# The experts' first layer in two fp16 parts, with a power-of-two scale of the weights formed on the chip

## The reference, cut to what matters

```python
logits = xt @ gate_w.T + gate_b
scores = softmax(logits); top_w, top_i = top_k(scores, 2)
def expert(w1e, b1e, w3e, b3e, w2e, b2e):          # each 256 x 256, 8 experts
    h = silu(xt @ w1e.T + b1e) * (xt @ w3e.T + b3e)
    return h @ w2e.T + b2e
y = sum over the two experts of a row, weighted by top_w
z = silu(xt @ ws1.T + bs1) * (xt @ ws3.T + bs3) @ ws2.T + bs2
```

## Time and profile before

| | |
|---|---|
| time, median of 3 runs | 591.88 us (591.18 to 594.17) |
| profiled execution: time, span | 593.51 us, 591.5 us |
| PE busy in the span | 562.3 us (95%) |
| PEld | 465.1 us (79%) |
| DVE | 452.1 us (76%) |
| ACT | 376.6 us (64%) |
| POOL | 257.5 us (44%) |
| mean granted TensorE clock | 0.984 |
| expert loop | 188 to 357 us |

### The profile page before, as it was taken

How to read it: one execution, slowest core, us unless ns; L and a number is a source line. 1 busy time by engine, 2 the same in 40 slices (tenths; PEclk the granted TensorE clock), 3 DMA queues, 4 the chain that set the end, 5 groups by cost and what they waited for, 6 DMA issues and landing times.

```text
span 591.5 us, 12910 instructions
## 1 busy us (share of the span) xinstructions
PE 562.3 (95%) x3942; PEld 465.1 (79%) x3942; DVE 452.1 (76%) x1246; ACT 376.6 (64%) x729; POOL 257.5 (44%) x291
## 2 busy tenths in 40 slices
PE   7989999999999999999999999979889999999997
PEld 7777998888879999999999997866646655655664
DVE  4778888886864877778888873757989899878765
ACT  5376887677634877777677753255575784785643
POOL 4427555565470234455443335667544651410100
PEclk9598999999999999999999999999999999999999
DMA  8225434562158878879998827453122330200000
GB/s 238 86 90 196 153 140 155 197 235 109 52 183 265 295 249 257 283 238 275 282 278 275 277 96 287 153 204 90 37 62 73 111 121 37 73 1 37 37 37 35
DMA packets 47973, 93.15 MB, mean 157 GB/s; under 512 B 6990, under 2 KB 17306, under 8 KB 47778
## 3 DMA queue, kind: packets, MB, share of 16 engines
q1 hardware_dynamic: 39740, 74.34, 37.5%
q0 software_dynamic: 7440, 17.97, 10.1%
q10 hardware_dynamic: 726, 0.02, 0.1%
HBM read 61.32 MB, written 32.17 MB: 158 GB/s over the span
## 4 chain that ended last, share of the span: by engine, by line
PE 61%; DVE 19%; ACT 9%; issue 6%; POOL 3%; DMA 1%; ACTq 0%; DVEq 0%; POOLq 0%; SPq 0%
PE bank L1363 13%; PE bank L1364 12%; PE bank L1365 12%; PE bank L1870 6%; PE bank L1301 4%; PE bank L1891 3%; PE bank L1893 3%; POOL yr L756 2%; DVE st L2447 2%; DVE xa L2438 2%; DVE g3l L2524 2%; DVE sl L2519 2%; DVE x L2081 2%; PE bank L1307 1%; PE bank L1330 1%
## 5 line engine op out<-in xcount | busy, mean ns | idle before, releaser
L660 POOL DMA_INDIRECT rows_by_expert<-n,pos x64 | 64.4, 1006 | 49.2 <-DVE pos L2175 32.7
L708 POOL TENSOR_TENSOR yg<-yg,b 128x512 f32<-128x512 f32 x31 | 45.9, 1481 | 89.6 <-ACT yg L848 89.6
L756 POOL DMA_INDIRECT yr<-expert_out,out_row x64 | 65.7, 1026 | 29.3 <-issue 19.0
L1363 PE MATMUL bank<-xTh,wph 128*128 128x256 f32 x248 | 72.3, 291 | 0.3 <-issue 0.2
L1870 PE MATMUL bank<-m4Th,wint 128*128 128x512 f16 x192 | 69.1, 380 | 2.6 <-DVE sl L2519 2.6
L1365 PE MATMUL bank<-xTh,wpl 128*128 128x256 f32 x248 | 70.1, 283 | 0.0
L1364 PE MATMUL bank<-xTl,wph 128*128 128x256 f32 x248 | 70.0, 282 | 0.0
L1870 PE MATMUL bank<-m4Tl,wint 128*128 128x512 f16 x192 | 68.8, 379 | 0.0
L2340 DVE TENSOR_TENSOR wpl<-wraw,wph 128x1024 fp32r<-128x1024 f32 x40 | 49.0, 1224 | 11.1 <-ACT wph L848 11.0
L848 ACT ACTIVATE wph<-wraw 128x1024 fp32r<-128x1024 f32 x40 | 42.4, 1059 | 14.6 <-PE bank L1365 9.7
L1363 PEld LDWEIGHTS bank<-xTh,wph 128*128 128x128 f32 x248 | 47.2, 190 | 0.6 <-issue 0.6
(11 more groups left out here) (352 smaller groups left out, 1727.1 us busy)
## 6 DMA issues: line engine op xcount, KB each, us to landing
wraw<-in_wexp SPq DMA_DIRECT2D x40, 512.0 KB, 4.6
xg<-rows_by_expert SPq DMA_DIRECT2D x31, 256.0 KB, 4.1
expert_out<-yg SPq DMA_DIRECT2D x31, 256.0 KB, 3.3
x_shared<-x SPq DMA_DIRECT2D x8, 512.0 KB, 3.1
xa<-x_shared SPq DMA_DIRECT2D x4, 1024.0 KB, 6.8
out<-ost SPq DMA_DIRECT2D x8, 512.0 KB, 2.7
xin<-in_x SPq DMA_DIRECT2D x7, 512.0 KB, 3.7
stage<-in_wexp SPq DMA_DIRECT2D x8, 256.0 KB, 3.6
```

The source lines that it names most:

```text
L660: pool.indirect_dma_start(out=xs, out_offset=bass.IndirectOffsetOnAxis(ap=pos[p][:, k, j:j + 1], axis=0), in_=n2[p][:, j, :], in_offset=No ...
L708: pool.tensor_tensor(yg[u % 3], yg[u % 3], b2[:, bass.ds(e, 1), :].broadcast_to([P, 2, D]), ALU.add)\
L756: pool.indirect_dma_start(out=yr[:, c, k, j, :], out_offset=None, in_=ys, in_offset=bass.IndirectOffsetOnAxis(ap=out_row[:, b * GB + c, k, ...
L1363: mm(o, ah, bh, start=first, stop=False)
```

## The change

`hidden(u)` gets both operands as fp16 parts. The rows are scaled by 2^11 (an immediate) and each expert's weights by a power of two, so that the largest stays within fp16 and the low parts don't vanish; the scale is taken off again in the silu's `scale` operand, in the split of `hb`, or for singles in `gated`. `outp` stays float32r. The scale comes from the mean square of an expert's first-layer weights: every expert's `wraw` is loaded once more, early, into one of two buffers `early`, and squared with an accumulated sum on ScalarE, one in steps 1 and 2 and two in steps 3, 4 and 5; TensorE sums over partitions in `biases()`, POOL raises to -0.5, VectorE keeps the exponent bits and forms the tables `wscale`, `unscale` and `b3c`. ScalarE and VectorE read the unit's expert before the weights' cast, no longer before silu and gate.

```diff
+        early = Area(area_a, top).put("early", [P, 2, KD, 2 * F], F32)
-        wph = [wa.put(f"wph{p}", [P, KD, 2 * F], F32R) for p in range(2)]
-        wpl = [wa.put(f"wpl{p}", [P, KD, 2 * F], F32R) for p in range(2)]
+        wph = [wa.put(f"wph{p}", [P, KD, 2 * F], F16) for p in range(2)]
+        wpl = [wa.put(f"wpl{p}", [P, KD, 2 * F], F16) for p in range(2)]
...
-        xTh = [ct.put(f"xTh{p}", [P, KD * P2], F32R) for p in range(2)]
+        xTh = [ct.put(f"xTh{p}", [P, KD * P2], F16) for p in range(2)]
...
+        def early_of(g):
+            return range(g - 1, g) if g < 3 else range(2 * g - 4, 2 * g - 2) if g < 6 else range(0)
...
                 if load:
                     load_x(g + 2, p)
+                for at, e in enumerate(early_of(g)):
+                    if early_of(g)[0]:
+                        sp.wait_ge(sem("norm_step"), early_of(g)[0])
+                    src = i["wexp"][e * (3 * P):e * (3 * P) + 2 * P, :].rearrange("(k p) n -> p k n", k=KD)
+                    sp.dma_start(early[:, at], src).then_inc(sem("early_in"), 16)
                 store_mid(g - 1, 1 - p)
...
                 scatter(f, 1 - p, (1,), second)
+                if g == 6:
+                    pool.wait_ge(sem("setup_copied"), 8)
+                    pool.tensor_scalar(wpow, wsum, SMALLEST, None, ALU.max).then_inc(sem("norm_step"), 1)
+                    pool.wait_ge(sem("norm_step"), NE + 1)
+                    pool.tensor_tensor(wpow, wpow, halfpow[:, 0:NE], ALU.pow).then_inc(sem("norm_step"), 1)
...
                 expert_high(g)
+                for at, e in enumerate(early_of(g)):
+                    act.wait_ge(sem("early_in"), 16 * (early_of(g)[-1] + 1))
+                    w = early[:, at].rearrange("p k n -> p (k n)")
+                    act.activation(w, w, ACT.Square, accum_out=wsq[:, e:e + 1]).then_inc(sem("norm_step"), 1)
...
             def weights_high(u):
+                at = tile_slot(u)
+                experts[u] = act.value_load(tile_expert[0:1, at:at + 1], min_val=0, max_val=NE - 1)
...
-                copy(wph[u % 2], wraw[u % 3]).then_inc(sem("high_done0"), 1)
+                copy(wph[u % 2], wraw[u % 3], scale_of(wscale, experts[u])).then_inc(sem("high_done0"), 1)
...
+            act.wait_ge(sem("table_done"), 1)
+            act.wait_ge(sem("norm_step"), NE + 4)
             weights_high(0)
...
-                copy(xTh[u % 2][:, 0:n], bank[:, 4 + u % 2, 0:n]).then_inc(sem("xTh_done"), 1)
+                copy(xTh[u % 2][:, 0:n], bank[:, 4 + u % 2, 0:n], ROW_SCALE).then_inc(sem("xTh_done"), 1)
...
-                        act.activation(hb[u % 2][:, n], bank[:, 2 * (u % 2), n], ACT.Silu,
+                        act.activation(hb[u % 2][:, n], bank[:, 2 * (u % 2), n], ACT.Silu, scale=scale_of(unscale, e),
...
-                    copy(hTh[u % 2], hb[u % 2]).then_inc(sem("hTh_done"), 1)
+                    copy(hTh[u % 2], hb[u % 2], scale_of(unscale, experts[u])).then_inc(sem("hTh_done"), 1)
...
                 pe.wait_ge(sem("shared_done"), pairs(5))
+                pe.wait_ge(sem("norm_step"), NE)
+                mm(bank[:, piece_bank(5, 0), 4 * NE:5 * NE], mean_of, wsq, start=True, stop=True)
...
+                if g == 7:
+                    dve.wait_ge(sem("norm_step"), NE + 2)
+                    chained(ts(wpow.bitcast(I32), wpow.bitcast(I32), EXPONENT, None, ALU.bitwise_and))
+                    chained(ts(wscale, wpow, LARGEST, None, ALU.mult))
+                    chained(ts(wpow, wscale, ROW_SCALE, None, ALU.mult))
+                    dve.reciprocal(unscale, wpow).then_inc(sem("norm_step"), 1)
+                    stt(b3c, b13c[:, 2:4, :], ROW_SCALE, wscale.unsqueeze(1).broadcast_to([P, 2, NE]), ALU.mult, ALU.mult)
...
-                tt(wpl[u % 2], wraw[u % 3], wph[u % 2], ALU.subtract).then_inc(sem("low_done0"), 1)
+                stt(wpl[u % 2], wraw[u % 3], scale_of(wscale, experts[u]), wph[u % 2], ALU.mult, ALU.subtract)
...
-                tt(xTl[u % 2][:, 0:n], bank[:, 4 + u % 2, 0:n], xTh[u % 2][:, 0:n], ALU.subtract).then_inc(sem("xTl_done"), 1)
+                stt(xTl[u % 2][:, 0:n], bank[:, 4 + u % 2, 0:n], ROW_SCALE, xTh[u % 2][:, 0:n], ALU.mult, ALU.subtract)
...
-                    tt(hTl[p], hb[p], hTh[p], ALU.subtract).then_inc(sem("hTl_done"), 1)
+                    stt(hTl[p], hb[p], scale_of(unscale, experts[u]), hTh[p], ALU.mult, ALU.subtract).then_inc(sem("hTl_done"), 1)
```

More of the change, by code:

```diff
@@ L35 @@
 HID_SCALE = 2.0 ** -19
+LARGEST = 2.0 ** 15 / 16
+SMALLEST = 1e-30
+EXPONENT = 0x7F800000
 ALU = mybir.AluOpType
@@ L105, in flamingo_kernel @@
         row_gap = keep.put("row_gap", [NE, 1], F32)
-        b13c = keep.put("b13c", [P, 4, NE], F32)
+        b13c = keep.put("b13c", [P, 5, NE], F32)
+        wsum = b13c[:, 4, :]
         incl = keep.put("incl", [NE, NE], F32)
@@ L130, in flamingo_kernel @@
         tile_row = keep.put("tile_row", [1, 2, NU], I32)
+        wsq = keep.put("wsq", [P, NE], F32)
+        wpow = keep.put("wpow", [P, NE], F32)
+        wscale = keep.put("wscale", [P, NE], F32)
+        unscale = keep.put("unscale", [P, NE], F32)
+        b3c = keep.put("b3c", [P, 2, NE], F32)
         area_a = keep.at
+        early = Area(area_a, top).put("early", [P, 2, KD, 2 * F], F32)
         wa = Area(area_a, top)
         wraw = [wa.put(f"wraw{p}", [P, KD, 2 * F], F32) for p in range(3)]
-        wph = [wa.put(f"wph{p}", [P, KD, 2 * F], F32R) for p in range(2)]
-        wpl = [wa.put(f"wpl{p}", [P, KD, 2 * F], F32R) for p in range(2)]
+        wph = [wa.put(f"wph{p}", [P, KD, 2 * F], F16) for p in range(2)]
+        wpl = [wa.put(f"wpl{p}", [P, KD, 2 * F], F16) for p in range(2)]
         wa.at = area_a + 2 * NE * KD * 2 * F * 4
@@ L212, in flamingo_kernel @@
         xg = [t.bitcast(F32) for t in xgr]
-        xTh = [ct.put(f"xTh{p}", [P, KD * P2], F32R) for p in range(2)]
-        xTl = [ct.put(f"xTl{p}", [P, KD * P2], F32R) for p in range(2)]
+        xTh = [ct.put(f"xTh{p}", [P, KD * P2], F16) for p in range(2)]
+        xTl = [ct.put(f"xTl{p}", [P, KD * P2], F16) for p in range(2)]
         hb, hbr = zip(*(ct.put_turned(f"hb{p}", [P, 2 * F]) for p in range(2)))
@@ L846, in _, with copy @@
         def _(act):
-            def copy(dst, src):
-                return act.activation(dst, src, ACT.Copy)
+            def copy(dst, src, scale=1.0):
+                return act.activation(dst, src, ACT.Copy, scale=scale)
             def stage_high(c, dst, n):
@@ L964, in biases_copy @@
                 act.wait_ge(sem("setup_mm"), 5)
-                copy(b13c.rearrange("p m e -> p (m e)"), bank[:, piece_bank(5, 0), 0:4 * NE]).then_inc(sem("setup_copied"), 1)
+                copy(b13c.rearrange("p m e -> p (m e)"), bank[:, piece_bank(5, 0), 0:5 * NE]).then_inc(sem("setup_copied"), 1)
             def step(g, p, nxt=True):
@@ L1032, in _, with scale_of @@
             f = NG - 1
+            experts = {}
+            def scale_of(table, e):
+                return table[:, bass.ds(e, 1)]
             def weights_high(u):
+                at = tile_slot(u)
+                experts[u] = act.value_load(tile_expert[0:1, at:at + 1], min_val=0, max_val=NE - 1)
                 act.wait_ge(sem(f"stage_in{u % 3}"), 16 * (EARLY[u % 3] + u // 3 + 1))
@@ L2336, in tile_tables, with scale_of @@
                         .then_inc(sem("table_done"), 1)
+            experts = {}
+            def scale_of(table, e):
+                return table[:, bass.ds(e, 1)]
             def weights_low(u):
+                at = tile_slot(u)
+                experts[u] = dve.value_load(tile_expert[0:1, at:at + 1], min_val=0, max_val=NE - 1)
                 dve.wait_ge(sem("high_done0"), EARLY[0] + u + 1)
-                tt(wpl[u % 2], wraw[u % 3], wph[u % 2], ALU.subtract).then_inc(sem("low_done0"), 1)
+                stt(wpl[u % 2], wraw[u % 3], scale_of(wscale, experts[u]), wph[u % 2], ALU.mult, ALU.subtract)\
+                    .then_inc(sem("low_done0"), 1)
             hidden(f, 0)
@@ L2357, in _ @@
             route_c(f)
+            dve.wait_ge(sem("table_done"), 1)
+            dve.wait_ge(sem("norm_step"), NE + 4)
             weights_low(0)
```

16 lines of the change are left out of this document (9 added, 7 removed).

## The result

The changed kernel takes 606.35 us (median of six, 601.12 to 607.97) where the one before takes 591.8 (median of six, 589.59 to 594.17): 1.0231 times as long, 95% interval 1.0196 to 1.0267. The forecast was 590.4, in a range up to 596.5; slower was given 0.20.

The account below looks back on a forecast made before the run. TensorE was taken to bound the expert loop, ScalarE's path to `probsT` the shared steps. Squares +6.05, clock +1.6, loop start +0.15 and matmuls -9.3 sum to -1.5 us: 590.4 from 591.88, range 586.5 to 596.5.

Parts of the forecast that it names:

- What bounds the kernel: Expert loop: TensorE sets the pace, matmuls 91.4% of the chain; shared steps: the path runs through ScalarE's `probsT`.
- Part 1, matmuls: Expert loop: fp16 hidden matmuls start every 0.1093 us, not 0.120; -9.3 us in all, bounds -9.9 and -7.8.
- Part 1, "Does another engine become the bound?": Expert loop: TensorE stays the bound; in a triple of about 11.15 us VectorE stands at 10.2, ScalarE near 9.8.
- Part 1, register loads: Expert loop: reads of the expert's number, moved ahead of the weight casts, run while their engine works; nobody waited there.
- Part 1, pointer operands: Expert loop: `[P,1]` operands cost ScalarE 0.09 us each, 0.36 per pair unit; VectorE's two between 0 and 0.09 each.
- Part 2, squares: End of steps 1 to 5 on ScalarE: eight squares of 1.05 us, after slack +6.05 us (5.0 to 7.5).
- Part 3, clock: Steps 4 to 6: longer TensorE idles bring two clock falls at 0.8 us each, +1.6 us (0 to 5.1).
- Part 4, "covered work", early loads: Shared steps: eight loads of 512 KB, queued on SP before `store_mid`, land half a step before their square; no cost.
- The wait of TensorE in `biases()`: Step 6: work behind the last square ends at 126.2 us, before `probsT` at 126.9; uncovered it would be 1.5 us.
- The expert loop doesn't follow TensorE: Rival, expert loop: late `wraw` landings hold triples at 11.81 us; 595.8, or 599.8 if all is held; chance 0.1.
- A table load for the square: Rival, shared steps: squares need their own table, five more loads of 1.28 us, +6.4 less slack; 596.4; chance 0.06.
- fp16 between fp32r matmuls: Rival, expert loop: fp16 streams no faster alternating with fp32r, gain 0 to 2 us; 598 to 600; chance 0.04.

Follow-up runs that it names:

- const_imm: const with immediates in place of pointer operands and the register loads back where they were before; 584.87 us, 0.9893 of before.
- const: The changed kernel without early loads, squares, product and power, scale tables filled with constants, register loads and pointer operands kept; 591.59 us, 0.9998 of before.
- const_reg: const, but ScalarE reads the expert of unit u + 2 ahead of silu_of(u), not behind it; 588.09 us, 0.9939 of before.
- squares: const plus the eight squares at the end of steps 1 to 5, on the data of only two early loads; 604.05 us, 1.0216 of before.
- warm8: The changed kernel with 8 spare products that TensorE issues in steps 2 to 6 while it waits for probsT; 616.50 us, 1.0283 of before.
- loads: const plus the eight early loads of 512 KB at their places in the steps, with no square reading them; 598.50 us, 1.0135 of before.
- first_dve: const, but a single's silu comes behind the next weights' cast on ScalarE, and VectorE reads the expert earlier; 596.68 us, 0.9925 of before.
- best: The changed kernel with squares in ScalarE's waits, loads behind the second norm, early register reads, singles' next cast ahead of silu; 596.34 us, 0.9933 of before.

## Why the prediction was wrong, point by point

- *The whole.* By the stretches, the result lies 15.3 us above the forecast: 9.9 in the loop, 5.0 in steps 1 to 6, 0.4 in the other two, the start left aside. Of the 5.0, squares are 2.2 (8.3 for 6.05), the clock 2.0 (3.6 for 1.6) and the last 0.8 fits step 3, where the wait for scatters is.
- *What bounds the kernel.* Right for before: TensorE paces the loop. Right too that the steps hang on ScalarE ahead of `probsT`.
- *Part 1, matmuls.* Right: 0.109 us apart, a pair unit 4.35 (forecast 4.38), and const_imm shows that triples can do better than the 11.15 forecast.
- *Part 1, "Does another engine become the bound?"* This is the step that failed in the loop. The prediction added up each engine's busy time in a triple (VectorE 10.2, ScalarE 9.8 of 11.15) and found slack. The true limit was a path through both, gate sum to silu to cast to low part to rows' low part, which had 1.22 us of slack in before; a TensorE faster by 0.7 to 1.1 a triple and a path longer by 0.70 use that up. Forecast -9.3, measured 0 (const); moving the register load alone gave 3.6 back (const_reg).
- *Part 1, register loads.* "They run in the queue while their engine works, and where they stood nobody waited": wrong, 0.38 us behind each single's silu. A load runs ahead only as far as the wait in front of it allows.
- *Part 1, pointer operands.* Right in size: `wph` 1.15 for 1.06, silu 0.56 for 0.47, `wpl` 1.28 for 1.22. They belong on the path, not in the busy sum.
- *Part 2, squares.* The length was right (1.04 for 1.05). This is the step that failed in the shared part: most of the slack taken off in steps 3 to 5 wasn't there. squares' step 3 grew by 2.1 us for its two squares, after's step 4 by 1.6, so nearly all of the 8.3 us count where 6.05 were taken; squares measured 12.8 with its falls. I read the reason from the order of work, and no run tests it: a step's start, values, residual, norm, softmax and next step's start close a circle, so a delay stays, and what looks early in one step of before is early only against a step that wasn't delayed.
- *Part 3, clock.* Two falls, as forecast, but some 1.8 us each and not 0.8: about 3.6 for 1.6, within the bounds given. The size is what steps 5 and 6 grew by beyond their squares; warm8 didn't settle it.
- *Part 4, "covered work", early loads.* Wrong: the loads were taken at 0, alone they cost 8 us (loads), and in after they show as 1.9 us of waits. I looked at which queue issued them and when they were wanted, not at whose transfers they stand beside. The wait of TensorE in `biases()` was 1.6 us, the "uncovered" value, and part of the idle ahead of step 6's fall.
- *Sums.* The lower bound of the matmuls' gain adds up to -10.1 us and not -9.9 (7.2, 1.2 and 1.7), and triples that keep 11.81 us for 11.15 would take back 5.9 and not 5.4. Neither decides anything.
- *Rivals.* "The expert loop doesn't follow TensorE" had the right outcome for the loop and the wrong mechanism: no wait for `wraw` in after's triples. It became true in const_imm, first_dve and best, where the ring was shortened. A table load for the square did not come, and fp16 between fp32r matmuls was fast. The time lay above all of them, because each assumed that only one half failed.

## What to carry to other kernels

When the engine that sets the pace gets faster, don't compare the others' busy sums with the new period: follow one item from engine to engine and compare the length of that path with it, waits for other engines included. An instruction that costs its engine nothing (a register read, a DMA issue) is priced by what stands behind it in the queue, and a transfer by what lands beside it. And work for an idle engine belongs where that engine waits: the squares cost 2.2% in front of the critical copy, and under 0.5%, loads included, in the waits of the next step.

## What of the hardware was new

- VectorE's `wpl` and GpSimd's bias addition, both with all inputs in SBUF, exclude each other, and a start 0.1 to 0.3 us earlier decides which one takes 1 us more: `wpl` 1.28 or 2.27, the addition 1.27 or 1.87 to 2.13.
- The same idle of 2.4 to 2.6 us ahead of the attention values brought 1.2 GHz for over 6 us in one step and nothing in another, in one execution (after, steps 5 and 4); squares, behind the same 2.55 us as after's step 4, had its longest fall there.
- The register read between silu and cast on ScalarE cost 0.38 us, and 0.68 in the triple behind it (silu at 313.63, cast at 314.63), though no row counts it as busy.
- Two loads of 512 KB issued beside a group's last scatters went with a wait of 0.9 to 3.7 us for their landing; issued 0.6 us or more behind the start of the last one, with at most 0.2.
